# A depthwise convolution as 32 by 32 products on the diagonal of TensorE's array, in a fused attention block

## What is computed

```python
x = x + conv(x, cond[:, None, :])      # depthwise, causal: 32 taps for each of 256 channels
ada = cond @ ada_w + ada_b             # six parts: shift1, scale1, gate1, shift2, scale2, gate2
x1 = ln(x) * (1 + scale1) + shift1
q, k, v = split(x1 @ qkv_w + qkv_b)    # 16 heads of 128
y = x + gate1 * (softmax(q k^T / sqrt(128)) v @ out_w + out_b)
x2 = ln(y) * (1 + scale2) + shift2
out = x + y + gate2 * (gelu(x2 @ ffn_w1 + b1) @ ffn_w2 + b2)
```

## Time and profile before

| what | us |
|---|---|
| median of 3 runs | 333.02 (331.53 to 333.71) |
| the profiled execution | 335.38 |
| its span, first to last instruction | 333.6 |
| TensorE busy in the span | 312.4 (94%) |
| VectorE, ScalarE, GpSimd busy | 152.3, 157.0, 76.8 |
| mean granted TensorE clock | 0.977 of full speed |

### The profile page before, as it was taken

The page is one execution under the profiler, slowest core; times in us unless marked ns, Lnnn a source line. Parts: engine busy times, 40 slices in busy tenths (PEclk is TensorE's granted clock), DMA queues, the critical chain, the costliest instruction groups (busy, mean ns, idle before and its releaser), DMA issues.

```text
span 333.6 us, 7533 instructions
## 1 busy us (share of the span) xinstructions
PE 312.4 (94%) x3279; PEld 266.4 (80%) x3279; DVE 152.3 (46%) x237; ACT 157.0 (47%) x258; POOL 76.8 (23%) x66
## 2 busy tenths in 40 slices
PE   4288999999999979999999999999999999899994
PEld 4288998988888858888888888888888687588884
DVE  6502382485344306225332532531625799783232
ACT  0723254655266243536625526644453647742910
POOL 5000076300053030014203005301102345420400
PEclk9699998999999998999999999999999999999999
DMA  4980023020033001003201001310100000000011
GB/s 142 265 305 4 4 76 115 3 65 0 2 82 109 0 8 59 2 0 121 69 0 39 24 0 63 96 34 0 65 2 1 2 2 0 0 2 0 0 65 63
DMA packets 10057, 15.74 MB, mean 47 GB/s; under 512 B 838, under 2 KB 6062, under 8 KB 9902
## 3 DMA queue, kind: packets, MB, share of 16 engines
q1 hardware_dynamic: 9600, 15.21, 14.5%
q10 hardware_dynamic: 429, 0.13, 0.2%
HBM read 14.26 MB, written 1.11 MB: 46 GB/s over the span
## 4 chain that ended last, share of the span: by engine, by line
PE 86%; DVE 7%; DMA 3%; issue 2%; SPq 0%; ACTq 0%; ACT 0%
PE bank L961 17%; PE bank L962 17%; PE bank L963 17%; PE bank L1037 8%; PE bank L869 5%; PE bank L970 5%; PE bank L971 4%; PE bank L972 4%; PE bank L1023 3%; PE bank L902 2%; PE bank L883 2%; DMA cond_padded<-zrows 2%; DMA toep<-cond_padded 2%; PE bank L938 2%; DVE yacc L763 1%
## 5 line engine op out<-in xcount | busy, mean ns | idle before, releaser
L293 POOL TENSOR_TENSOR wl<-raw,wh 128x512 fp32r<-128x512 f32 x40 | 52.6, 1337 | 168.9 <-ACT wh L355 168.9
L961 PE MATMUL bank<-x1h,wl 128*128 128x512 f32 (+1 forms) x176 | 67.3, 383 | 0.0
L424 ACT ACTIVATE pool<-bank,bg 128x512 f32<-128x512 f32 x56 | 38.6, 689 | 58.3 <-PE bank L963 58.1
L962 PE MATMUL bank<-x1l,wh 128*128 128x512 f32 (+1 forms) x176 | 65.8, 374 | 0.0
L963 PE MATMUL bank<-x1h,wh 128*128 128x512 f32 (+1 forms) x176 | 65.8, 374 | 0.0
L680 DVE SCALAR_TENSOR_TENSOR ol<-bank,bT,oh 128x512 fp32r<-128x512 f32 x32 | 24.0, 750 | 49.9 <-ACT oh L453 48.9
L961 PEld LDWEIGHTS bank<-x1h,wl 128*128 128x128 f32 x176 | 33.9, 192 | 6.0 <-issue 0.6
L962 PEld LDWEIGHTS bank<-x1l,wh 128*128 128x128 f32 x176 | 34.0, 193 | 5.6 <-issue 0.2
L963 PEld LDWEIGHTS bank<-x1h,wh 128*128 128x128 f32 x176 | 33.9, 192 | 5.7
L1037 PEld LDWEIGHTS bank<-pt,pool 128*128 128x128 f32 x256 | 31.9, 191 | 3.4 <-DVE pt L669 0.8
L1037 PE MATMUL bank<-pt,pool 128*128 128x128 f32 x256 | 32.8, 276 | 0.6 <-DVE ol L680 0.4
(11 more groups left out here) (107 smaller groups left out, 442.2 us busy)
## 6 DMA issues: line engine op xcount, KB each, us to landing
raw<-in_L_cond_qkv_w_dram SPq DMA_DIRECT2D x12, 512.0 KB, 3.9
raw<-in_L_cond_out_w_dram SPq DMA_DIRECT2D x4, 512.0 KB, 3.6
raw<-in_L_cond_ffn_w_dram SPq DMA_DIRECT2D x4, 512.0 KB, 3.4
pool<-in_x_dram SPq DMA_DIRECT2D x2, 512.0 KB, 4.6
toep<-cond_padded SPq DMA_DIRECT2D x4, 256.0 KB, 4.5
adaw<-in_L_cond_ada_w_dram SPq DMA_DIRECT2D x1, 1024.0 KB, 8.3
out_dram<-pool SPq DMA_DIRECT2D x4, 256.0 KB, 2.2
adaw<-in_L_cond_ada_w_dram SPq DMA_DIRECT2D x1, 512.0 KB, 6.2
```

What stands on the lines that cost most here:

```text
L293: g.tensor_tensor(wl[:, cols], raw[:, cols], wh[:, cols].bitcast(F32), ALU.subtract)\
L424: a.activation(dst, src, ACT.Identity, bias=bg[:, j // GH, j % GH:j % GH + 1])\
L961: pe.matmul(dst, wl[:, w_cols], a_hi, start=start, stop=False)
L962: pe.matmul(dst, wh[:, w_cols], a_lo, start=False, stop=False)
```

## The change

The four zero blocks of the Toeplitz tile go. `toep` is now `[128, 64 slots, 32]`: group `j`'s matrices are on its own 32 partitions only. A product reads 32 rows by 32 columns of it (`toep[T*j:T*(j+1), c, :]`) and 32 rows of `xq`, at place (j, j) of the array, so the count of products is as before, 256. Both operands are contiguous: the loads go to `toep_in`, and four copies of 128 by 512, two on DVE and two on ACT, turn them block by block to `toep`. The moving operand is read in the order (i n), so the sequences come in another order, and `turn` picks their columns accordingly. `conv_out` has the slots innermost, so its copies write with a stride of 64 words and the weights of `turn` are contiguous. The 16 copies to `xq` are shared by three engines: DVE 8, ACT 4, POOL 4. The bias loads and the first part of the modulation weights are issued by SP ahead of the Toeplitz loads, and the scratch writes come first on ACT. The modulation is in three parts of 8 products: before the convolution, before `turn(3)`, and inside the first chunk's projections. ACT splits the first four pieces of the weights before `xc_copy(0)`.

```diff
-        with nc.sbuf_tensor("conv_out", [P, SLOTS, B], F32) as conv_out:
+        with nc.sbuf_tensor("conv_out", [P, B, SLOTS], F32) as conv_out:
...
+        toep = pool[:, 0:2048].rearrange("p (s u) -> p s u", u=T)
+        xq = pool[:, 4096:6144].rearrange("p (s i n) -> p s i n", s=SLOTS, i=QB)
+        toep_in = pool[:, 2048:4096].rearrange("p (u s) -> p u s", u=T)
...
-        SPREAD_BY_ACT = [(i, g) for g in range(QB) for i in range(QB)][1::3]
+        SPREADS = [(i, g) for g in range(QB) for i in range(QB)]
+        SPREADS_ACT, SPREADS_POOL = SPREADS[0::4], SPREADS[2::4]
+        SPREADS_DVE = SPREADS[1::2]
...
-        ADA_PARTS = [(0, ADA1), (ADA1, ADA)]
-        ADA_BANKS = [YB[1], YB[1]]
+        ADA_PARTS = [(0, ADA1), (ADA1, 2 * ADA1), (2 * ADA1, ADA)]
+        ADA_BANKS = [YB[1], OB[1], YB[1]]
...
@@ scalar
+            a.wait_ge(s_toep, 16 * QB)
+            for k in (1, 3):
+                blk = slice(CBLK * k, CBLK * (k + 1))
+                a.activation(toep[:, blk, :].rearrange("p s u -> p u s"), toep_in[:, :, blk], ACT.Copy)\
+                    .then_inc(s_tp[k], 1)
             conv_copy(0)
             conv_copy(2)
+            high_parts(0, range(0, 4))
             xc_copy(0)
+            group_biases(0, 0, 3)
             squares(0)
             xc_copy(2)
-            group_biases(0, 0, 3)
-            high_parts(0, range(0, 2))
+            high_parts(0, range(4, 6))
             squares(1)
-            high_parts(0, range(2, 4))
             x1_high(0)
-            high_parts(0, range(4, 6))
...
@@ vector
+            v.wait_ge(s_toep, 16 * QB)
+            for k in (0, 2):
+                blk = slice(CBLK * k, CBLK * (k + 1))
+                v.tensor_copy(toep[:, blk, :].rearrange("p s u -> p u s"), toep_in[:, :, blk]).then_inc(s_tp[k], 1)
+            v.wait_ge(s_btc, 1)
+            modulation(0)
+            one_plus(0, SCALE1)
             conv_copy(1)
             conv_copy(3)
...
@@ tensor
+                pe.wait_ge(s_tp[k], 1)
                 for s in range(CBLK):
                     c = CBLK * k + s
                     for j in range(QB):
-                        m = pe.matmul(CB[k][T * j:T * (j + 1), B * s:B * (s + 1)], toep[:, j, :, c],
-                                      xq[:, c, :, :].rearrange("p i n -> p n i"), start=True, stop=True)
+                        m = pe.matmul(CB[k][T * j:T * (j + 1), B * s:B * (s + 1)], toep[T * j:T * (j + 1), c, :],
+                                      xq[T * j:T * (j + 1), c, :, :].rearrange("p i n -> p (i n)"),
+                                      start=True, stop=True)
...
-                        m = pe.matmul(tiles[T * q:T * (q + 1), :, b, :], conv_out[:, s0:s0 + T, XB_B * n + b],
+                        m = pe.matmul(tiles[T * q:T * (q + 1), :, b, :], conv_out[:, col, s0:s0 + T],
```

More of the change, by code:

```diff
@@ L110, in cond_resid_block_kernel @@
         vt = sb("vt", [P, TG, T])
-        with nc.sbuf_tensor("toep", [P, QB, T, SLOTS], F32) as toep:
-            pass
         hh = sb("hh", [P, MT, HT], F32R)
@@ L399, in _ @@
                 a.wait_ge(s_x[n], 16)
-            for i, g in SPREAD_BY_ACT:
+            for i, g in SPREADS_ACT:
                 a.activation(xq[T * g:T * (g + 1), :, i, :],
@@ L726, in _ @@
             x1_low(0)
+            modulation(1)
             scale_up(1)
@@ L732, in _ @@
             x1_low(1)
+            modulation(2)
+            one_plus(2, SCALE2)
             centre(2)
-            modulation(1)
-            one_plus(1, SCALE2)
             scale_up(2)
@@ L941, in modulation @@
                 m.then_inc(s_adap, 1)
+            pe.wait_ge(s_cond, 1)
+            pe.wait_ge(s_adaw[0], 16)
+            modulation(0)
+            pe.wait_ge(s_xq[0], len(SPREADS_ACT))
+            pe.wait_ge(s_xq[1], len(SPREADS_DVE))
+            pe.wait_ge(s_xq[2], len(SPREADS_POOL))
+            for k in range(NX):
+                conv(k)
             turn(0)
@@ L1077, in _ @@
             spread(1)
-            project_chunk(0, (2, 3))
+            project_chunk(0, (2,))
+            pe.wait_ge(s_co[1], 2)
+            modulation(2)
+            project_chunk(0, (3,))
+            pe.wait_ge(s_adat, ADA_STEPS[1])
             mean(2)
```

68 lines of the change are left out of this document (28 added, 40 removed).

## The result

In fifteen runs of each kernel on one chip, taken in turn, the changed kernel has a median of 334.72 us (331.48 to 335.84) and the kernel before 332.65 us (329.21 to 336.48). The ratio is 1.007, with a 95% interval of 1.0041 to 1.0100. The change makes the kernel 0.7% slower, inside the 1% that the prediction calls no change. The forecast of 328.7 us and its range, to 333.5, are missed.

The account below looks back on a forecast made before the run. It took the serial chain before the first projection (48.72 us) and TensorE's full stretch after it as the bound. Projection 6.2 us sooner, third modulation +1.9, net -4.3 from the 333.02 median: 328.7 us, range 321.5 to 333.5.

Parts of the forecast that it names:

- 10.9 us from mean(0) to the first projection: Norm chain: 12.6 us before, less 1.1 for the first modulation and 0.6 for turn 2; projection at 42.5.
- Rival A: Convolution and turns: instructions arrive in time, no such holes; net -10.9 us, 322.1 us; chance 0.15.
- Rival C: Spreads: POOL's copies delay the convolution; gain gone at 2.4 us a copy, 337 us at 3.4; chance 0.08.
- D: Whole kernel: nothing measurable, Toeplitz lands 3 to 4 us later behind bias and modulation loads; 332 us; chance 0.10.
- B: TensorE to the projections: clock stays low or 32-row products take 24 ns; 330.2, or 331 to 332 us; chance 0.19.
- the 0.5: Convolution: some 0.5 us runs before the next 16 KB request, making 2.9 us per further 128 records.
- The start: First convolution product at 16.4 us: Toeplitz landing 14.7, delay 0.9, turning copy 0.8.
- the spreads' 0.9: Before the convolution: copies to xq on DVE, ACT and POOL delay its start by 0.9 us.
- The first block: Convolution: 187 records at hand last to 19.0 us; the next 16 KB of instructions comes at 21.9.
- The two further blocks: Convolution: two more 128-record instruction blocks at 2.9 us each, reaching 27.7 us.
- The last burst and the copy behind it: Convolution's end: last 69 records 0.7 us, to 28.4; last strided copy 0.9, to 29.3.
- The turns: Turns 0 and 1: 59 records at hand, next 16 KB at 30.6, the rest 1.0 us; mean(0) at 31.6.

Follow-up runs that it names:

- late_bulk: Changed kernel with the second modulation and projection weight loads held until two convolution blocks are done; 333.14 us, 1.0034 of the kernel before.
- mod_early: Changed kernel with the third modulation moved from inside the projections to behind var(1); 332.17 us, 0.9939 of the kernel before.
- woven: mod_early plus POOL's first four low parts ahead of rstd(0) and the second modulation between convolution blocks 0 and 1; 329.18 us, 0.9872 of the kernel before.
- warm: Changed kernel with two wide products, results unused, ahead of the convolution; 334.78 us, 1.0077 of the kernel before.
- single: Kernel before with one product of 128 strided weight columns in place of four of 32; 344.94 us, 1.0371 of the kernel before.
- one_pass: Changed kernel with convolution operands rounded to bf16, one record per product instead of two, less exact; 326.95 us, 0.985 of the kernel before (2 runs).
- toep_first: Changed kernel with Toeplitz loads again ahead of the modulation weights and bias loads on ACT; 336.83 us, 1.0132 of the kernel before.

## Why the prediction was wrong

**Right.** That the gain is decided before the first projection; that compact products run like the score products at the full clock (64 records in half a microsecond, 63 for the scores) and slower at the lower level, 14 ns (14.7); that the clock did not make the 30 ns of before; that the bursts run into holes of "issue" with a 16 KB transfer before each, after 187 records (186); 10.9 us from mean(0) to the first projection (10.75); the third modulation as 1.87 us among the projections (+1.7 in that stretch); a start at 16.4 (17.00). One reading behind this was off: the 33 ns given for the stretch to 18.95 us is 30 by its row (141 records in 4.24 us), which changes no term. Rival A, instructions in time, is excluded by every trace. Rival C, slow POOL copies, too: 1.08 us each and over six microseconds before they are needed. D, at a chance of 0.10, named what came, no change to speak of, but by luck: the Toeplitz load landed 1.5 us later and not 3 to 4, and the rest was lost in the convolution. B's clock came true up to 37 us and its slow products didn't.

**The step that failed** is in the part on the convolution: "Every further 128 records cost the 2.4 us plus what runs before the next request, some 0.5: 2.9 us", with the first block at 21.9. The term's mechanism holds, its size was too small, and the part that was mis-sized is the 0.5. The 2.4 us are the time from the start of a block's transfer to the resume of TensorE, and they held in every fetch of the table below. What was put at 0.5 is the time from the entry into the block before to the start of that transfer. From queue views of 0.1 us (the entry is the start of the row or, marked "about", worked out from the pace of its records):

| trace | block before entered | transfer starts | TensorE resumes | entry to transfer | transfer to resume | GB/s beside it |
|---|---|---|---|---|---|---|
| before | about 17.1 | 20.1 | 22.53 | 3.0 | 2.4 | 388 |
| changed | about 17.8 | 21.4 | 23.76 | 3.6 | 2.4 | 391 |
| changed | 23.76 | 24.9 | 27.11 | 1.1 | 2.2 | under 40 |
| changed | 27.11 | 28.2 | 30.72 | 1.1 | 2.5 | 8 |
| late_bulk | about 17.5 | 18.3 | 20.73 | 0.8 | 2.4 | 5 |
| late_bulk | 20.73 | 22.3 | 24.62 | 1.6 | 2.3 | 0 |
| late_bulk | 24.62 | 28.4 | 30.70 | 3.8 | 2.3 | 377 |

With quiet DMA the first wait is 0.8 to 1.6 us, beside the bulk loads 3.0 to 3.8; the second is the same in both cases (up to 2.8 in mod_early). So the loads delay the start of the transfer. By its pieces, to mean(0) at 31.6 forecast and 36.64 measured (+5.0):

- The start, +0.6: the turning copy took 0.8 as forecast (first of two in 1.08), but the load landed at 16.2 and not 14.7; the spreads' 0.9 fell away beside it.
- The first block, +1.3 more: 23.76 for 21.9. late_bulk, without the loads, resumed at 20.73. The 2.4 us of the earlier trace rows came from a fetch in quiet DMA, and this one ran beside 350 GB/s. The traces of before had it: there the block entered after 75 records (203 less 128, at 17.1 us by 32 ns each) was followed only at 22.53, 5.4 us on, beside 401 GB/s; here it is 5.9 us, from 17.85 to 23.76. I didn't price it.
- The two further blocks, +1.2: 3.35 and 3.61 us from resume to resume for 2.9. In woven, where these blocks meet little other traffic, they are 3.32 and 3.34. That is the least in these traces; with quiet DMA too it goes up to 3.9 (warm, mod_early), and why it differs stays open.
- The last burst and the copy behind it, +0.6: 71 records in 1.18 us (17 ns each) for 0.7, and the copy 1.0 for 0.9.
- The turns, +1.3: 3.64 us for 128 records where 1.0 was forecast after a wait for their block. They run at the lower clock, 28 ns a record, while turn 2 at the full clock takes 17 (1.10 for 64). The clock stayed low to 37 us. That the holes kept it there isn't shown: in single TensorE had none, and it stayed low too.

With the floor in place of 2.9 the result follows from the trace of before. After its first resume the old convolution needed 9.40 us for 309 records; at 3.4 us for each of two full blocks and 17 ns for each of the last 53 records (0.9) they need 7.7. Only 1.7 us was to be had there (1.26 came: 8.14 us, for 326 records), and 1.1 us came up to the resume (6.76 us from the start for 7.82). These 2.3 us paid for the later start and for nothing else; the slow turns and the 1.87 us in the full stretch were paid by the shortened norm chain (2.1 us), and nothing was left.

The Trainium skill ("Runtime: NRT & Kernel Launch", section "Instruction fetch mechanics") calls the crossing of a 16 KB boundary mostly hidden. At the old pace of 3.8 us a block the trace agrees from 22.53 us on, though not at 21.16, beside the loads; at 1.9 us a block there was a hole at each one.

## What to carry to other kernels

Before making small TensorE products faster, count instructions: straight-line code of 256 instructions should hold at least 3.4 us of work, and 5.3 to 6.1 us where loads of 350 to 400 GB/s run beside it (as measured here), and what is faster than that turns into "issue". Save instructions rather than nanoseconds (one_pass), and where a late fetch can't be avoided, put needed slow products into it (woven). A step moved into the stretch where the engine is never idle is paid in full. Before the clock column is trusted early in a span, compare it with the pace of products that are known at both levels.

## What the runs showed that was not expected

- Entered straight ahead, 256 TensorE instructions come every 3.3 to 3.4 us at best (woven 3.32 and 3.34), and 6.08 us passed from resume to resume beside 377 GB/s (late_bulk).
- The pace of compact 32-column products follows the clock (64 records in half a microsecond at 1.00, 41 at 0.50, in late_bulk), as that of the modulation does (1.87 us for 16 records, 3.62 at the lower level); that of the strided products of before doesn't (30 ns at either level). In one_pass a bf16 record takes 10 ns at 0.50.
- Bulk loads lengthen the wait before the transfer of an instruction block starts (0.8 to 1.6 us with quiet DMA, 3.0 to 3.8 beside the loads), and not the 2.2 to 2.5 us from there to the resume.
- The same late fetch at 122 us is a hole of about 2 us in some kernels (before, changed, late_bulk) and absent in others (toep_first, mod_early); what decides it was not tried, and it is worth about what the medians of the two kernels differ by.
- An engine busy without a gap is no sign that its clock rises: single stayed at 1.2 GHz for 28 us of strided weight loads.
- Large loads issued ahead of a small dependent one move it: the pads landed at 9.31 instead of 7.98 behind 512 KB of modulation weights, and at 7.75 in toep_first, where these weights come later.
- POOL working beside DVE made two of DVE's steps cost 2.71 and 1.82 us instead of 0.75 and 0.76.
